# Fused early-fusion block on one core: values and softmax sums from one product per head, swapped by two transfers

## The reference

```
h = concat([tok(x), txt], axis=1)                     # 32 x 165 x 256
# attention on layernorm(h): 16 heads of 16
att = (q @ k.T) / sqrt(16)
att = where(mask == 0, -inf, att); att = softmax(att)  # mask: key <= query and key % 4 != 3
h = h + (att @ v) @ Wp + bp
# experts on layernorm(h): 8 experts choose 660 of the 5280 tokens each
probs = softmax(xn @ router_w.T + router_b); gates, idx = top_k(probs.T, 660)
ye = gelu(xe @ fc1_w.T + fc1_b) @ fc2_w.T + fc2_b
h = h + scatter_add(ye * gates) / max(scatter_add(gates), 1e-9)
```

## Time and profile before

| | |
|---|---|
| median of 3 runs | 859.29 us |
| profiled execution | 859.55 us, its span 857.7 us |
| TensorE busy | 744.2 us, 87% |
| VectorE busy | 573.1 us, 67% |
| ScalarE busy | 397.3 us, 46% |
| GpSimd busy | 374.7 us, 44% |
| granted TensorE clock, mean | 0.928 of full |

### The profile page before, as it was taken

How to read it: one execution, slowest core, us unless ns; L and a number is a source line. 1 busy time by engine, 2 the same in 40 slices (tenths; PEclk the granted TensorE clock), 3 DMA queues, 4 the chain that set the end, 5 groups by cost and what they waited for, 6 DMA issues and landing times. The chain is left out here.

```text
span 857.7 us, 18735 instructions
## 1 busy us (share of the span) xinstructions
PE 744.2 (87%) x6840; PEld 673.3 (78%) x6840; DVE 573.1 (67%) x1343; ACT 397.3 (46%) x857; POOL 374.7 (44%) x504
## 2 busy tenths in 40 slices
PE   3699999999999999999997511379999999999994
PEld 2577888888888888888885411369999999999994
DVE  1135777668768768667664378776787787887561
ACT  0214455454455455455443155035557366475570
POOL 3113464464465454465444223023537347355334
PEclk9899999999999999999998755569999999999998
DMA  8952675555774675475661342011344453442122
GB/s 273 307 96 48 89 117 97 86 104 98 108 119 99 94 99 96 103 119 99 96 90 51 94 149 74 29 28 43 72 132 64 117 144 49 127 102 32 34 32 32
DMA packets 80686, 82.36 MB, mean 96 GB/s; under 512 B 36161, under 2 KB 74943, under 8 KB 80244
## 3 DMA queue, kind: packets, MB, share of 16 engines
q1 hardware_dynamic: 67980, 66.92, 38.8%
q0 software_dynamic: 11584, 10.96, 8.2%
q10 hardware_dynamic: 1032, 3.30, 1.1%
HBM read 34.59 MB, written 16.22 MB: 59 GB/s over the span
## 5 line engine op out<-in xcount | busy, mean ns | idle before, releaser
L595 POOL DMA_INDIRECT out<-r_arena x48 | 80.3, 1674 | 118.2 <-DVE r_arena L1530 107.9
L656 ACT ACTIVATE r_arena<-ps_all 126x660 f32<-126x660 f32 x128 | 92.2, 720 | 56.9 <-PE ps_all L879 55.3
L1249 DVE RECIPROCAL r_arena<-ps_all 128x165 f32<-128x165 f32 x64 | 76.1, 1189 | 61.3 <-PE ps_all L894 61.3
L520 POOL TENSOR_SCALAR_AFFINE_SELECT r_arena<-r_arena 126x660 f32<-126x660 f32 x128 | 97.0, 767 | 45.9 <-ACT r_arena L656 45.5
L1238 DVE TENSOR_REDUCE mx<-ps_all 128x4 f32<-128x504 f32 (+1 forms) x160 | 105.0, 669 | 15.3 <-PE ps_all L856 13.8
L879 PE MATMUL ps_all<-Qp,Kp 98*126 98x166 f32 x512 | 84.6, 289 | 7.9 <-ACT r_arena L656 6.1
L856 PE MATMUL ps_all<-Kp,Qp 96*65 96x56 f32 (+1 forms) x512 | 90.6, 293 | 0.0
L1552 DVE TENSOR_TENSOR hT_lo<-r_arena,hT_hi 128x330 fp32r<-128x330 f32 x128 | 63.2, 502 | 39.8 <-ACT r_arena L760 39.6
L582 POOL DMA_INDIRECT xe<-xn_rows,r_arena x48 | 59.8, 1245 | 63.4 <-issue 36.5
L1111 PE MATMUL ps_all<-xeT_hi,W_hi 128*128 128x330 f32 x256 | 83.1, 325 | 1.1 <-DVE hT_lo L1552 1.1
L758 ACT ACTIVATE hT_hi<-ps_all,vec_s 128x330 fp32r<-128x330 f32 x128 | 68.9, 539 | 32.4 <-PE ps_all L1111 30.1
(11 more groups left out here) (178 smaller groups left out, 1706.6 us busy)
## 6 DMA issues: line engine op xcount, KB each, us to landing
H<-w SPq DMA_DIRECT2D x16, 1024.0 KB, 5.6
Qp<-q_hi SPq DMA_DIRECT2D x64, 166.0 KB, 3.9
Kp<-k_hi SPq DMA_DIRECT2D x128, 63.0 KB, 4.1
Qp<-q_lo SPq DMA_DIRECT2D x32, 166.0 KB, 4.7
out<-H SPq DMA_DIRECT2D x16, 330.0 KB
xn_rows<-r_arena SPq DMA_DIRECT2D x16, 330.0 KB
Kp<-k_lo SPq DMA_DIRECT2D x64, 63.0 KB, 4.1
H<-h SPq DMA_DIRECT2D x1, 3360.0 KB, 22.6
```

The source lines that it names most:

```text
L520: pool.affine_select(PT[0:S, g, :, :], PT[0:S, g, :, :], [[0, 4], [STEP - 1, T]], ALU.is_ge, 0.0, base=STEP - 2, channel_multiplier=-STEP) ...
L595: pool.indirect_dma_start(rows_out, bass.IndirectOffsetOnAxis(tok[0:A, e % NTB, a:a + 1], 0), yw[0:A, a, :], None, bounds_check=NTOK - 1, ...
L656: act.activation(PT[0:S, g, :, :].rearrange("p (k h) t -> p k h t", k=2), pair[:, :, :, 0:T], ACT.Exp, scale=float(HD) ** -0.5).then_inc(e ...
L1249: dve.reciprocal(rS[:, c, :], bank(2 + c)[:, T:2 * T]).then_inc(rs_sum, 1)
```

## The change

One product per head now gives both values and sums. V holds for each head 32 columns in which value columns and ones alternate: value, one, value, one for the first head of a strip, and one, value, one, value for the second. The first head's product goes to columns 0 to T of the bank, the second's to columns T to 2T, so the second group of products with ones is gone. ScalarE masks the second head's rows by parity into `other`, once for the odd rows (its values) and once for the even rows (its sums). VectorE merges: even rows of the first head plus the masked values give the values of both heads interleaved (`y_val`), odd rows plus the masked sums give the sums (`y_inv[:, 0]`), and it takes the reciprocal of those in place. A value and its inverse then lie in neighbouring partitions. Two transfers by SyncE, one for even and one for odd partitions, swap neighbours into `y_inv[:, 1]`. GpSimd multiplies values and inverses into yT, one round later, behind select 1. The packed keys have their two head halves in another order, and Wp and the value bias are permuted on the host.

```diff
-        rS = cut(R_ARENA, KD, T)
+        other = cut(R_ARENA, KD, 2, T)
-            Qp, Kp = sb1("Qp", [128, 3, HC, TE], F32R), sb1("Kp", [128, 3, HC, 2, S], F32R)
+            Qp, Kp = sb1("Qp", [128, 3, HC, TE], F32R), sb1("Kp", [128, 3, 2, HC, S], F32R)
-            V = sb1("V", [128, 3, 2, 272])
+            V = sb1("V", [128, 3, NH, HD, 2])
+            y_val, y_inv = sb1("y_val", [128, KD, T]), sb1("y_inv", [128, 2, KD, T])
+        def value_columns_of(v):
+            return bass.AP(v.tensor, v.offset, [list(v.ap[0]), [4 * HD, HC], [2 * HD + 1, 2], [2, HD]])
...
@@ SyncE, behind pack_max(b + 1) and ahead of store_h
+            def move_heads(b):
+                sp.wait_ge(y_inverse, 2 * b + 2)
+                for side in range(2):
+                    sp.dma_start(y_inv[side:128:2, 1], y_inv[1 - side:128:2, 0]).then_inc(y_moved, 16)
@@ GpSimd, for image b - 1, in every round behind zero_future(b, 1); for the last image at b == B
+            def heads_out(b, c):
+                n, u = divmod(b, 2)
+                pool.wait_ge(y_moved, 32 * b + 32)
+                if n >= 2 and c == 0 and u == 0:
+                    pool.wait_ge(proj_done, RT * (n - 2) + RT)
+                pool.tensor_tensor(yT[:, n % 2, c, u * T:(u + 1) * T], y_val[:, c, :], y_inv[:, 1, c, :], ALU.mult)\
+                    .then_inc(yT_ready, 1)
@@ ScalarE, at the end of round b
+            def mask_heads(b, c):
+                act.wait_ge(pv_done, 2 * b + c + 1)
+                if b >= 1:
+                    act.wait_ge(y_merged, 4 * b + 2 * c - 2)
+                for i in range(2):
+                    act.activation(other[:, c, i, :], bank(2 + c)[:, T:2 * T], ACT.Identity,
+                                   scale=kf("even_odd")[:, 1 - i:2 - i]).then_inc(y_masked, 1)
@@ TensorE, mix_values
-                    pe.wait_ge(yT_ready, 2 * b + c - 1)
+                    pe.wait_ge(y_merged, 4 * b + 2 * c - 2)
                 for w in range(2):
-                    for part in range(2):
-                        for j in range(4):
-                            dst = bank(2 + c)[32 * j:32 * j + 32, part * T:(part + 1) * T]
-                            lhs = v_rows(b % 3, w, 4 * c + j)[0:S] if part == 0 else ones_eo[0:S, w, :]
-                            mm = pe.matmul(dst, lhs, PT[0:S, 2 * c + w, j, :], start=(w == 0 and part == 0),
-                                           stop=(w == 1), skip_group_check=True)
+                    for j in range(4):
+                        mm = pe.matmul(bank(2 + c)[32 * j:32 * j + 32, w * T:(w + 1) * T],
+                                       V[0:S, b % 3, 2 * (4 * c + j) + w].rearrange("p d o -> p (d o)"), PT[0:S, 2 * c + w, j, :], start=(w == 0),
+                                       stop=(w == 1), skip_group_check=True)
@@ VectorE, in the place of heads_out
-                dve.reciprocal(rS[:, c, :], bank(2 + c)[:, T:2 * T]).then_inc(rs_sum, 1)
-                dve.tensor_tensor(yT[:, n % 2, c, u * T:(u + 1) * T], bank(2 + c)[:, 0:T], rS[:, c, :], ALU.mult)\
-                   .then_inc(yT_ready, 1)
+            def invert(b, c):
+                dve.wait_ge(y_masked, 4 * b + 2 * c + 2)
+                if b >= 1:
+                    dve.wait_ge(yT_ready, 2 * b + c - 1)
+                for i, dst in enumerate((y_val[:, c, :], y_inv[:, 0, c, :])):
+                    dve.scalar_tensor_tensor(dst, bank(2 + c)[:, 0:T], kf("even_odd")[:, i:i + 1], other[:, c, i, :],
+                                             ALU.mult, ALU.add).then_inc(y_merged, 1)
+                dve.wait_ge(y_merged, 4 * b + 2 * c + 2)
+                dve.reciprocal(y_inv[:, 0, c, :], y_inv[:, 0, c, :]).then_inc(y_inverse, 1)
```

More of the change, by code:

```diff
@@ L414, in _ @@
                     pack_max(b + 1)
+                if 0 <= b < B:
+                    move_heads(b)
                 if u == 1 and 0 <= n - 1 < NPAIR:
@@ L448, in _ @@
                 if i == 0:
-                    zero(V[:, :, :, :])
+                    pool.memset(V[:, :, :, :, :], 1.0).then_inc(pinit_done, 1)
             def rstd1(n):
@@ L521, in zero_future @@
                                    base=STEP - 2, channel_multiplier=-STEP).then_inc(causal_done, 1)
+            def heads_out(b, c):
+                n, u = divmod(b, 2)
+                pool.wait_ge(y_moved, 32 * b + 32)
+                apart(pool)
+                if n >= 2 and c == 0 and u == 0:
+                    pool.wait_ge(proj_done, RT * (n - 2) + RT)
+                    apart(pool)
+                pool.tensor_tensor(yT[:, n % 2, c, u * T:(u + 1) * T], y_val[:, c, :], y_inv[:, 1, c, :], ALU.mult)\
+                    .then_inc(yT_ready, 1)
             pool.wait_ge(cf_in, 16)
@@ L527, in _ @@
                 has_s = 0 <= b < B
+                if b == B:
+                    heads_out(b - 1, 0)
+                    heads_out(b - 1, 1)
                 if u == 0:
@@ L712, in _ @@
                     copy_xn2T(n - 1)
+                if 0 <= b < B:
+                    mask_heads(b, 0)
+                    mask_heads(b, 1)
             act.wait_ge(sm_shift, 1)
@@ L856, in row_scores @@
                     mm = pe.matmul(dst[0:rows, 2 * j * cols:2 * (j + 1) * cols].rearrange("p (w s) -> p w s", w=2),
-                                   Qp[0:MROW, q, h, at_row:at_row + rows], Kp[0:MROW, q, h, :, 0:cols],
+                                   Qp[0:MROW, q, h, at_row:at_row + rows], Kp[0:MROW, q, :, h, 0:cols],
                                    start=False, stop=(j == len(pairs) - 1), skip_group_check=True)
@@ L878, in key_scores @@
                         h = 4 * (g // 2) + 2 * k + j
-                        mm = pe.matmul(dst[0:S, j * TE:(j + 1) * TE], Kp[0:MROW + 2, q, h, g % 2, :],
+                        mm = pe.matmul(dst[0:S, j * TE:(j + 1) * TE], Kp[0:MROW + 2, q, g % 2, h, :],
                                        Qp[0:MROW + 2, q, h, :], start=(j == 0), stop=(j == 1), skip_group_check=True)
@@ L1310, in round_of @@
                 if has_s:
-                    heads_out(b, 0)
-                    heads_out(b, 1)
+                    invert(b, 0)
+                    invert(b, 1)
                 if u == 1 and has_p:
@@ L1625 @@
     perm = np.arange(D).reshape(HC // 2, KD, 2, HD).transpose(1, 2, 3, 0).reshape(D)
-    minus = np.zeros((2, HC, 2, S), f4)
+    mixed = np.arange(D).reshape(HC, 2, HD).transpose(0, 2, 1).reshape(D)
+    minus = np.zeros((2, 2, HC, S), f4)
     for w in range(2):
-        minus[w, :, w] = -1.0
+        minus[w, w] = -1.0
     x = a["x"].reshape(B, CH, IMG // PATCH, PATCH, IMG // PATCH, PATCH)
@@ L1647 @@
         "minus": minus,
-        "watt": np.stack([rows(attn("Wq")[:, perm]), rows(attn("Wk")[:, perm]), rows(attn("Wv")), rows(attn("Wp"))],
+        "watt": np.stack([rows(attn("Wq")[:, perm]), rows(attn("Wk")[:, perm]), rows(attn("Wv")), rows(attn("Wp")[mixed])],
                          axis=1),
-        "vecs": np.concatenate([cols(attn("bq")[perm]), cols(attn("bk")[perm]), cols(attn("bv")),
+        "vecs": np.concatenate([cols(attn("bq")[perm]), cols(attn("bk")[perm]), cols(attn("bv")[mixed]),
                                 cols(a["L0_ffn_fc1_b"].reshape(-1)),
```

36 lines of the change are left out of this document (14 added, 22 removed).

## The result

The changed kernel took 961.24 us (median of 4, 960.29 to 964.49), beside 858.95 (857.87 to 859.64) for the kernel before on the same chip: 1.121 times as long, 95% interval 1.1188 to 1.1232. That is +102, where +77.5 was forecast. The direction, the order of events and most steps came out as forecast; one cost, TensorE's clock, did not.

What follows compares the result with a forecast made beforehand. Bound taken: a loop in which TensorE, VectorE and GpSimd hand work to each other, 25.51 us a pair. Terms 60 + 1.5 + 8.4 + 7.6 = 77.5 on 859.55 gave 937 us; range 895 to 972.

Steps and rivals of the forecast that it cites:

- nothing comes back: TensorE's removed matmuls, 1.13 us a round or 36 us in all, would shorten nothing, since other engines set the pair.
- Maskings 395, merges 381, reciprocal 1.19, products 0.47 to 0.52: Costs per instruction: ScalarE masking 395 ns, VectorE merge 381 ns alone, reciprocal from SBUF 1.19 us, GpSimd product 0.47 to 0.52.
- Rival 3: VectorE's reciprocal from SBUF costs only 0.67 us, saving 2.1 us a pair: 905 us; 10%.
- The loop's four edges: Even mix to statistics 5.34 us, on to odd mix 8.47, to even statistics 5.43, to the projection 7.95.
- The order on GpSimd as the largest step: Even round: projection waits for products queued behind add_bp and second select; statistics to mix 11.3 us, not 9.10: +2.2.
- The swap: SyncE's two 84 KB transfers land 4.8 us behind the last reciprocal, hidden in both rounds, barely in the odd one.
- Rival 4: Swap lands later or GpSimd's products cost more (at 0.8 us, +1.2 a pair): 955 to 975 us; 15%.
- Projection to mix, 3.30 in every pair: Even round: from the projection's start to the mix stays 3.30 us, as in the kernel before.
- rival 5: TensorE's clock falls in the new waits: +26 us if half the pairs slow, up to 977; 4%.
- The small terms: First pair +1.5 us, pairs ending at images 28 and 30 +4.2 each, last mix +2.0, way out behind it +5.6.
- Rival 1: TensorE sets the time, so its 36 us are returned in whole: 823 to 830 us; 7%.
- rival 2: The steps are there but half hidden by slack in the loop: +2.5 us a pair, 890 to 905; 10%.

Runs made afterwards that it cites:

- half-mix experiment: The kernel before with half of its mixing matmuls left out and nothing added; 849.21 us, 0.990 times the kernel before.
- first experiment: The changed kernel with GpSimd's two products of even rounds moved from behind the second select to ahead of the first; 907.48 us.
- filled kernel: The changed kernel with unread 180-column matmuls, seven calls ahead of the projection's wait and five ahead of odd rounds' third row-score group; 941.43 us.
- the kernel with the deferred even image: The changed kernel with separate buffers by image parity, even images' reciprocals, swap and products later, odd images' products heading the even round; 868.33 us.

## Why the prediction was right, and what it mis-sized

- **Group of eight, four groups a round off TensorE: right; "nothing comes back": right in direction.** Even alone they are worth 10 us, not 36 (half-mix experiment).
- **Maskings 395, merges 381, reciprocal 1.19, products 0.47 to 0.52:** 396, 340 to 381, 1190 ns, 475 ns. Rival 3 is refuted: the reciprocal costs from SBUF what it costs from PSUM. The line drawn from two rows held. The rule of the Trainium skill on faster SBUF modes (VectorE: DVE Perf Modes, The perf-mode tier table) did not show in it.
- **The loop's four edges:** 5.10, 8.57, 5.14, 7.90 for 5.34, 8.47, 5.43, 7.95. The two behind a mix were 0.2 to 0.3 too dear: I took both the maskings and the merges in whole, and the experiment without them shows a little over half of that on the path.
- **The order on GpSimd as the largest step: right.** Its two instructions ahead of the selects return 54 us; 2.2 a pair would have given about 33 for 15 pairs, and the clock's part of the same wait makes most of the difference (an estimate: 907.5 against 941.4 without the clock's part leaves 34).
- **The swap: hidden, as said, but mis-sized in itself.** It lands 2.0 us after issue; I had 4.1 to 4.6 from the packings' rows, which are twice as large or scattered otherwise. Rival 4 fell with it (products at 475 ns, swap earlier and not later). The last image shows the difference: product 8.5 us and projection 9.4 behind the mix, not 11.7. I had this term 2.3 too high.
- **Projection to mix, 3.30 in every pair, was the failed term.** It measured 5.0 to 6.35 in the twelve pairs between the mixes of images 2 and 26, and 3.30 where nothing waits (first experiment). Over these pairs that is 28 us more than twelve times 3.30; the other edges gave 3 back, so that the pairs came out 25 us over the sum's 60. That is the whole miss of 24. I had written this down as rival 5, with the place, the wait of 2.3 us (2.25 measured) and the price of +26, and gave it 4%. It is what happened: a fall in every one of these pairs, full in half of them and partial in the others. The ground given, that in the earlier trace rows no fall is seen, was no ground: there TensorE waited 0.3 us in all, and the change adds a wait of 2 us to every pair. A row of a state that the change abolishes can't vouch for the new one. The only row in a state like the new one was the earlier trace rows. It showed 0.50, and TensorE had waited just before it:

```profile
468.94 1.14 PE L879 MATMUL ps_all<-Qp,Kp 98*126 98x166 f32 x4 [4.03 <-ACT r_arena L656]
```

The Trainium skill, TensorE: Matmul & The Clock Gate (HAM oscillation), describes a loop whose waits set the clock back in each of its rounds; the waits in its example are about 3 to 5 us. The trace agrees, and for shorter ones: a fall behind twelve of the thirteen waits of 1.9 to 2.3 us. I cited it and didn't let it weigh.

- **The small terms nearly cancel, which is luck.** The first pair was to cost 1.5 because it "has no projection". That is a misreading: round 2 projects the first pair, TensorE waits 2.29 us ahead of it, and the pair cost 4.5. The pairs that end at images 28 and 30 cost 2.2 and 7.1, for 4.2 each; the last mix 1.9 for 2.0; the way out 3.3 for 5.6. The last projection, at the low clock, took 5.45 us instead of 2.81, which the sum did not have, and the first mix came 2.7 us earlier than before.
- **The range.** It held 961 because its upper part was kept for rival 4, a later swap or dearer products, and neither came. Rival 5, which did, was to be left out of it at its upper end.
- **The other rivals.** Rival 1 fell with the first bracket on L934, rival 2 with the pair of 32.6: no step was half hidden.

Left open: why the clock falls behind some waits and not behind their like. It stayed at 1.00 behind the first wait of 2.29 us in the changed kernel; in the filled kernel it fell in seven odd rounds behind a wait of 0.77 us and not in the others; and single rounds of the first experiment are 17.4 and 16.9 beside 15.3. The runs show that taking away or filling the long wait gives the clock back in most rounds.

## What to carry to other kernels

Where several engines are level, take the loop's edges one by one from the time line: relieving the busiest engine gives back only the gap to the next (10 of 36 us here), and a new stop in an in-order queue is paid each round by whoever stands behind it. When a change puts a wait of microseconds ahead of TensorE, price the work behind the wait at the low clock too, and look for a row in which TensorE has really waited. Before adding a step to GpSimd's or SyncE's queue, write down who waits for each entry behind the place: a move helps only if it passes no other waiter.

## What the runs showed of the chip

- Behind twelve of thirteen waits of 1.9 to 2.3 us, in a stage where TensorE is otherwise mostly busy, the next 6.4 us were granted 0.52 to 0.57 (six times) or 0.73 (six times). Filling the waits with matmuls that nobody reads, 63.6 us of busy time, made the kernel 20 us faster.
- 82.5 KB from SBUF to SBUF, every other partition, landed 2.0 us after issue; 63.0 KB in packings 4.1 us in the kernel before and 3.8 with the keys' new order. The Trainium skill, DMA: Bandwidth & Descriptors (Anatomy of one DMA), gives about 2.0 us as the fixed cost, for another path of issue; the swap agrees with that, the packings don't.
- The time to issue a transfer varies: two packings were issued in 1.23 us and in 2.62 (the kernel with the deferred even image). With the stores moved away single ones still took up to 1.56, where 0.60 is usual.
- A matmul call on plain float32 data stands in the trace as two matmuls; a filling of eight calls of 256 columns took 3.64 us. The four calls of a key score group, in the fast float32 format, stand there as four.
